# Gate and up as three float32r products with split weights and tokens, and the route's inverse roots as Newton rounds on VectorE

## The reference, cut to what matters

```python
def rmsnorm(x, w): return x * rsqrt(mean(x * x, -1, keepdims=True) + EPS) * w
h = rmsnorm(x, mlp_norm_w)
x = x + (silu(h @ Wgate) * (h @ Wup)) @ Wdown          # 128 -> 512 -> 128

# second mixture of experts, on x = layernorm of the sum so far
xn = (x - mu) * rsqrt(var + LN_EPS) * gamma + beta
probs = softmax(xn @ Wr + br); scores, idx = top_k(probs, 2)   # 8 experts
```

## Time and profile before

| what | us |
|---|---|
| runs: median (lowest to highest of 3) | 1336.76 (1336.28 to 1343.72) |
| the profiled execution's own time | 1339.15 |
| its span, first to last instruction | 1336.8 |
| PE busy in the span | 1201.7 |
| DVE busy in the span | 914.6 |
| ACT busy in the span | 829.8 |
| POOL busy in the span | 505.1 |
| mean granted TensorE clock | 0.958 |

### The profile page before, as it was taken

The page is one execution under the profiler, slowest core; times in us unless marked ns, Lnnn a source line. Parts: engine busy times, 40 slices in busy tenths (PEclk is TensorE's granted clock), DMA queues, the critical chain, the costliest instruction groups (busy, mean ns, idle before and its releaser), DMA issues. The chain is left out here.

```text
span 1336.8 us, 26862 instructions
## 1 busy us (share of the span) xinstructions
PE 1201.7 (90%) x7787; PEld 913.1 (68%) x7787; DVE 914.6 (68%) x3538; ACT 829.8 (62%) x2478; POOL 505.1 (38%) x619
## 2 busy tenths in 40 slices
PE   6999999999999998699975999999996989199990
PEld 4766676666667665499963777777774656199990
DVE  6788888888888775444436888888873666244445
ACT  5898888888989885244432565566554666044440
POOL 2111324142424232455542343433432376545550
PEclk9999999999999999799997999999997999599995
DMA  9100000000000000222221000000000011222226
GB/s 294 49 2 1 12 7 11 7 13 8 16 5 13 8 11 5 80 67 71 71 77 41 17 16 17 16 1 1 1 1 1 13 40 40 79 61 71 70 73 195
DMA packets 54443, 52.91 MB, mean 40 GB/s; under 512 B 7341, under 2 KB 43098, under 8 KB 54330
## 3 DMA queue, kind: packets, MB, share of 16 engines
q1 hardware_dynamic: 36320, 29.39, 7.7%
q0 software_dynamic: 8928, 17.84, 4.0%
q10 hardware_dynamic: 9082, 4.33, 1.1%
HBM read 29.48 MB, written 22.05 MB: 39 GB/s over the span
## 5 line engine op out<-in xcount | busy, mean ns | idle before, releaser
L1356 ACT ACTIVATE prob<-prob,negmax 128x256 f32<-128x256 f32 (+3 forms) x512 | 283.2, 556 | 37.5 <-DVE negmax L1450 37.5
L1450 DVE CUSTOM_DVE_ANT_0 prob<-bank,mask 128x256 f32<-128x256 f32 (+3 forms) x512 | 224.6, 480 | 36.8 <-PE bank L1166 34.4
L1529 POOL TENSOR_TENSOR Vs<-Vh_sb,rinv 128x512 f32<-128x512 f32 x64 | 66.7, 1042 | 355.9 <-DVE rinv L1428 355.9
L1052 POOL DMA_INDIRECT expert_out<-f_x_yb,f_x_to x142 | 136.8, 963 | 153.4 <-DVE f_x_yb L1040 131.0
L1178 PE MATMUL bank<-prob,Vs 128*64 128x512 f32 (+3 forms) x1024 | 153.6, 443 | 2.9 <-POOL Vs L1529 2.8
L680 POOL DMA_INDIRECT expert_in<-f_xn,f_slot x128 | 126.4, 987 | 46.2 <-issue 30.8
L984 PE MATMUL bank<-f_x_xbT,W_sb 128*128 128x256 f32 x568 | 138.6, 388 | 1.6 <-DVE f_x_xbT L1020 1.5
L1005 ACT ACTIVATE f_x_hid<-bank,cols 128x256 f32<-128x256 f32 x144 | 63.8, 475 | 91.4 <-PE bank L984 91.4
L984 PEld LDWEIGHTS bank<-f_x_xbT,W_sb 128*128 128x128 f32 x568 | 104.6, 194 | 14.8 <-DVE f_x_xbT L1020 2.6
L1178 PEld LDWEIGHTS bank<-prob,Vs 128*64 128x64 f32 x1024 | 64.2, 137 | 72.7 <-issue 62.9
L1005 ACT ACTIVATE prob<-bank,cols 128x256 f32<-128x256 f32 x140 | 62.1, 474 | 82.8 <-PE bank L984 82.8
(11 more groups left out here) (263 smaller groups left out, 3169.1 us busy)
## 6 DMA issues: line engine op xcount, KB each, us to landing
f_x_xb<-expert_in SPq DMA_DIRECT2D x73, 130.0 KB, 2.2
b_crows<-expert_out SPq DMA_DIRECT2D x16, 256.0 KB, 2.8
c_crows<-expert_out SPq DMA_DIRECT2D x16, 256.0 KB, 4.2
expert_out<-f_x_yb,f_x_to POOLq DMA_INDIRECT x142
expert_in<-fill ACTq DMA_DIRECT2D x16, 130.0 KB, 3.6
x_sb<-in_L_attn_a_x_dram SPq DMA_DIRECT2D x8, 256.0 KB, 6.4
W_sb<-in_L_ffn_W_dram SPq DMA_DIRECT2D x1, 2048.0 KB, 10.0
expert_in<-f_xn,f_slot POOLq DMA_INDIRECT x128, 2.4
```

The source lines that it names most:

```text
L1052: pool.indirect_dma_start(yg, bass.IndirectOffsetOnAxis(ap=self.to[:, t:t + 1], axis=0), self.yb[:, t, :], None).then_inc(self.stored[t], 16)
L1356: nc.scalar.activation(mine, mine, ACT.Exp, scale=-1.0, bias=negmax[:, g % 2, i, a:a + 1], accum_out=rowsum[:, g % 2, i, a:a + 1]).then_in ...
L1450: nc.vector.tensor_tensor_reduce(out=prob[:, g % 2, a, columns(i)], in0=score_bank(i, a), in1=mask[:, T - width[i]:], scale=-1.0, scalar=H ...
```

## The change

In the MLP stage:

- Gate and up become `matmul3` on float32r parts. The weights are split once, at the start of the stage, by four DVE instructions; ACT's `evacuate` writes the high part of the tokens, and DVE makes the low part in a new step `low_x(b)`, for row 0 before the loop and for row b + 1 between `gated(b,2)` and `gated(b,3)`. PE's `turn` and the start of a row wait for the low part instead of the high one.
- The two roots of a row leave POOL. DVE computes them in `dve_power`, directly behind `dve_base`: a start value from the bits of the base (a shift, then a multiply-add on integers), and three Newton rounds of three instructions each, on 128x8 elements, each instruction waiting for the one before. DVE's first `gated` of the next row stands behind them.

```diff
+            def dve_power(self, dve, b, u):
+                base = self.power[:, u, 2:4, :]
+                y = [self.root[:, k, :, :] for k in range(2)]
+                step = START + b * self.ROOT_STEPS
+                dve.wait_ge(self.base, START + 2 * b + 2)
+                nc.vector.tensor_scalar(self.root_bits[:, :, :], base.bitcast(i32), 1, None,
+                                        ALU.logical_shift_right).then_inc(self.rooted, 1)
+                dve.wait_ge(self.rooted, step + 1)
+                nc.vector.tensor_scalar(y[0].bitcast(i32), self.root_bits[:, :, :], -1.0, float(0x5F3759DF),
+                                        ALU.mult, ALU.add).then_inc(self.rooted, 1)
+                for r in range(self.ROUNDS):
+                    done = step + 2 + 3 * r
+                    out = self.power[:, u, 4:6, :] if r == self.ROUNDS - 1 else y[(r + 1) % 2]
+                    dve.wait_ge(self.rooted, done)
+                    nc.vector.tensor_tensor(self.root_square[:, :, :], y[r % 2], y[r % 2],
+                                            ALU.mult).then_inc(self.rooted, 1)
...
+                    ins.then_inc(self.rooted if r < self.ROUNDS - 1 else self.rstd, 1)
+                dve.sem_inc(self.rooted, 1)
...
-                            nc.tensor.matmul(bankG[c % 2][:, :], Wgate_sb[:, c * P:(c + 1) * P], xnT[:, b % 2, :],
-                                             start=True, stop=True).then_inc(gate_done, 1)
+                            f = slice(c * P, (c + 1) * P)
+                            matmul3(bankG[c % 2][:, :], Wgate_hi[:, f], Wgate_lo[:, f], xnT_hi[:, b % 2, :],
+                                    xnT_lo[:, b % 2, :]).then_inc(gate_done, 1)
...
                         turn(0)
+                        pe.wait_ge(gate_up_low, 2)
                         for b in range(B):
-                            pe.wait_ge(xnT_ready, START + b + 1)
+                            pe.wait_ge(xnT_lo_ready, START + b + 1)
...
+                        for high, full in ((Wgate_hi, Wgate_sb), (Wup_hi, Wup_sb)):
+                            nc.vector.tensor_copy(high[:, :], full[:, :]).then_inc(gate_up_high, 1)
...
+                            nc.vector.tensor_tensor(low[:, :], full[:, :], high[:, :],
+                                                    ALU.subtract).then_inc(gate_up_low, 1)
                         route.dve_begin(dve)
+                        def low_x(b):
+                            dve.wait_ge(xnT_ready, START + b + 1)
+                            nc.vector.scalar_tensor_tensor(
+                                out=xnT_lo[:, b % 2, :], in0=bankT[:, :], scalar=mlp_norm_col, in1=xnT_hi[:, b % 2, :],
+                                op0=ALU.mult, op1=ALU.subtract).then_inc(xnT_lo_ready, 1)
...
                             route.norm.dve_base(dve, b, slot_of(b))
+                            route.norm.dve_power(dve, b, slot_of(b))
...
                             gated(b, 2)
+                            if b < LAST:
+                                low_x(b + 1)
                             gated(b, 3)
...
-                            route.norm.pool_power(pool, b - 1, slot_of(b - 1))
...
-                        route.norm.pool_power(pool, LAST, slot_of(LAST))
```

More of the change, by code:

```diff
@@ L309, in __init__ @@
                     self.base, self.terms = sem(name + "_base_ready", at), sem(name + "_terms_ready", at)
-                    self.of_dve = (self.stats, self.moments, self.xn, self.base, self.terms)
-                self.of_pool = (self.pool_step, self.rstd, *[s for s in (self.sum, self.htok) if s is not None])
+                    self.rooted = sem(name + "_root_step", at)
+                    self.root = sb(name + "_root", [P, 2, 2, NT], at=at)
+                    self.root_square = sb(name + "_root_square", [P, 2, NT], at=at)
+                    self.root_error = sb(name + "_root_error", [P, 2, NT], at=at)
+                    self.root_bits = sb(name + "_root_bits", [P, 2, NT], i32, at=at)
+                    self.of_dve = (self.stats, self.moments, self.xn, self.base, self.terms, self.rstd, self.rooted)
+                self.of_pool = () if lean else (
+                    self.pool_step, self.rstd, *[s for s in (self.sum, self.htok) if s is not None])
             def tiles(self, b, where=None):
@@ L361, in dve_base @@
                                         ALU.add).then_inc(self.base, 1)
[L363 to L367, removed]
+            ROUNDS = 3
+            ROOT_STEPS = 2 + 3 * ROUNDS
@@ new lines, in dve_power @@
+            def dve_power(self, dve, b, u):
[14 more added lines that the diff above has]
+                                            ALU.mult).then_inc(self.rooted, 1)
+                    dve.wait_ge(self.rooted, done + 1)
+                    nc.vector.scalar_tensor_tensor(out=self.root_error[:, :, :], in0=self.root_square[:, :, :],
+                                                   scalar=-0.5, in1=base, op0=ALU.mult,
+                                                   op1=ALU.mult).then_inc(self.rooted, 1)
+                    dve.wait_ge(self.rooted, done + 2)
+                    ins = nc.vector.scalar_tensor_tensor(out=out, in0=self.root_error[:, :, :], scalar=1.5, in1=y[r % 2],
+                                                         op0=ALU.add, op1=ALU.mult)
+                    ins.then_inc(self.rooted if r < self.ROUNDS - 1 else self.rstd, 1)
+                dve.sem_inc(self.rooted, 1)
@@ L2011, in mlp_stage @@
                 xn = sb("m_xn", [P, 2, NT, D], at=st)
-                xnT = sb("m_xnT", [P, 2, T], at=st)
+                xnT_hi, xnT_lo = sb("m_xnT_hi", [P, 2, T], f32r, at=st), sb("m_xnT_lo", [P, 2, T], f32r, at=st)
+                Wgate_hi, Wgate_lo = sb("Wgate_hi", [P, INTER], f32r, at=st), sb("Wgate_lo", [P, INTER], f32r, at=st)
+                Wup_hi, Wup_lo = sb("Wup_hi", [P, INTER], f32r, at=st), sb("Wup_lo", [P, INTER], f32r, at=st)
+                gate_up_high, gate_up_low = sem("m_gate_up_high", st), sem("m_gate_up_low", st)
+                xnT_lo_ready = sem("m_xnT_lo_ready", st)
                 silu = sb("silu", [P, 2, T], at=st)
@@ L2046, in hidden @@
                             pe.wait_ge(silu_ready, START + n - 1)
-                            nc.tensor.matmul(bankG[c % 2][:, :], Wgate_sb[:, c * P:(c + 1) * P], xnT[:, b % 2, :],
-                                             start=True, stop=True).then_inc(gate_done, 1)
+                            f = slice(c * P, (c + 1) * P)
+                            matmul3(bankG[c % 2][:, :], Wgate_hi[:, f], Wgate_lo[:, f], xnT_hi[:, b % 2, :],
+                                    xnT_lo[:, b % 2, :]).then_inc(gate_done, 1)
                             pe.wait_ge(act_ready, START + n - 1)
-                            nc.tensor.matmul(bankU[c % 2][:, :], Wup_sb[:, c * P:(c + 1) * P], xnT[:, b % 2, :],
-                                             start=True, stop=True).then_inc(up_done, 1)
+                            matmul3(bankU[c % 2][:, :], Wup_hi[:, f], Wup_lo[:, f], xnT_hi[:, b % 2, :],
+                                    xnT_lo[:, b % 2, :]).then_inc(up_done, 1)
                         def down(b):
@@ L2101, in evacuate @@
                             act.wait_ge(turned, START + b + 1)
-                            nc.scalar.activation(xnT[:, b % 2, :], bankT[:, :], ACT.Copy,
+                            nc.scalar.activation(xnT_hi[:, b % 2, :], bankT[:, :], ACT.Copy,
                                                  scale=mlp_norm_col).then_inc(xnT_ready, 1)
@@ L2135, in _ @@
                     def _(dve):
-                        begin(dve, act_ready, x_done, *route.of_dve, *experts.of_dve)
-                        route.dve_begin(dve)
+                        begin(dve, act_ready, x_done, xnT_lo_ready, *route.of_dve, *experts.of_dve)
+                        for high, full in ((Wgate_hi, Wgate_sb), (Wup_hi, Wup_sb)):
+                            nc.vector.tensor_copy(high[:, :], full[:, :]).then_inc(gate_up_high, 1)
+                        for k, (low, full, high) in enumerate(((Wgate_lo, Wgate_sb, Wgate_hi),
+                                                               (Wup_lo, Wup_sb, Wup_hi))):
+                            dve.wait_ge(gate_up_high, k + 1)
+                            nc.vector.tensor_tensor(low[:, :], full[:, :], high[:, :],
+                                                    ALU.subtract).then_inc(gate_up_low, 1)
+                        route.dve_begin(dve)
+                        def low_x(b):
[3 more added lines that the diff above has]
+                                op0=ALU.mult, op1=ALU.subtract).then_inc(xnT_lo_ready, 1)
                         def x_add(b):
```

3 lines of the change are left out of this document (2 added, 1 removed).

## The result

The changed kernel takes 1364.14 us (median of four runs, 1361.17 to 1367.53), the kernel before on the same chip 1337.09: ratio 1.0188 with a 95% interval of [1.0161, 1.0215], slower. The forecast was 1352 with a range to 1360; the direction came out, and the time is 12 us above it, beyond the range.

A forecast was written before the change was run, and what follows sets the result against it. A chain through several engines, not PE, was taken to bound the MLP rows. 1339.15 + 11.3 (rows +11.4, start -0.5, tail +0.4) + 4.4 for the clock = 1354.9, on the median's base 1352; range 1341 to 1360.

The forecast's parts named there:

- The bound: MLP rows: a chain through several engines sets each row at 13.30 us; PE is merely nearly as long.
- Products: Gate and up on PE: a triple saves 0.17 us, one per row on the path; N to x_add becomes 8.63.
- N: Moment in each row when DVE comes to the normalising step: 4.50 us behind x_add before, 6.80 forecast.
- the rival with a triple no cheaper: Gate and up: a triple takes 1.29 us, N to x_add is 0.6 longer, total 1356; chance 0.05.
- Roots: DVE before gated(b,0): eleven dependent steps at 0.20 us, 2.20 in all; everything behind moves by 2.30.
- Low part of the tokens: DVE between gated(b,2) and gated(b,3): one instruction per row, 0.75 us, hidden while DVE waits for PE.
- Start: Weight split and row 0: PE's first product 1.2 us later, triples then save; net -0.5, between -1.5 and +2.5.
- Tail: Row 7's slots and scatters: +0.4 us, since DVE's root takes 2.4 from L360 to N instead of POOL's 2.0.
- Clock: PE's pauses in MLP rows: clock falls cost 1.1 us in four of seven intervals, +4.4, ends 0 and 13.
- clock falls in every row: MLP rows: the case of a clock fall in each row, left out of the range 1341 to 1360.

The follow-up runs named there:

- the products alone: Against the changed kernel, the roots go back to POOL and the float32r triples stay: 1335.78 us, ratio 0.9977.
- the filled pause: Against the changed kernel, ten unread float32r products in rows 1 to 7 between gate and up of chunk 2: 1351.53 us, ratio 1.0095.
- the roots alone: Against the kernel before, the Newton roots on DVE as in the change, gate and up left as float32 products: 1350.13 us, ratio 1.0091.
- the one with the sum later: Against the changed kernel, POOL's addition of z to x for the last row moved behind its next wait: 1362.16 us, ratio 1.0169.
- the exponential first and the pause filled: Against the products alone, ACT's exponential ahead of the update of x, and five unread products before the next row's transposes: 1338.0 us, ratio 0.9994.

## Why the prediction was wrong

The forecast before rounding was 1352.5, and 1364.1 came: 11.7 more. The profiled execution accounts for 6.3 of them. Against the working its seven intervals are 3.6 longer, the start 1.45 and the tail 0.2, behind the scatters 1.65 came, and the part outside the span is 0.6 shorter. The other 5.4 lie between that execution and the median: I carried over -2.39, but the profiled execution of the changed kernel was its fastest run, and the median lies 2.97 above it.

**The bound: right.** The rows are set by a chain through all engines and not by PE. The products alone took 6 us off PE's busy time in the seven intervals and nothing off their sum.

**Products: right.** N to x_add was put at 8.63. It is 8.59 and 8.66 in the two intervals of the changed kernel without a fall, and 8.60 to 8.84 in the whole rows of the filled one. In the rival with a triple no cheaper the 3.9 for row 0 does not follow from its rows: eight triples at 1.29 instead of 0.69 are 4.8, which makes that rival 1357.

**Roots: right.** The step was put at 0.20 and is 0.20; N was put at 6.80 behind x_add and is 6.82. The sum of the intervals without the clock was put at 108.3, +11.4; the pause filled gives 109.33, +12.4. The five whole rows there are 15.44 to 16.07 long, where I had put 15.43 for each. The Trainium skill ("VectorE: DVE Perf Modes", section "The DRAIN you can't avoid") finds, on eight copies, that a semaphore behind each costs nothing extra. That does not carry over to tiles this small: a step would then be its duration, 0.17 here, and it is 0.20, while the two independent bases L365 and L366 lie 0.08 apart (1107.54 and 1107.62).

**Low part of the tokens: right.** It takes 0.74, and N to x_add is as forecast with it, so it is hidden.

**Start: wrong by 1.45.** Forecast -0.5, measured +0.95, inside its ends of -1.5 and +2.5. I had left out that POOL's addition runs beside DVE's second subtraction, which costs 1.07 there (1.75 against 0.68). The Trainium skill has this in "SBUF — State Buffer", section "Who interferes with whom": a VectorE instruction with two inputs in SBUF and a GpSimd instruction that reads SBUF exclude each other, and the one that starts second waits for the whole of the other. The traces agree nearly: POOL began at 1024.54 and DVE, at 1024.63, was the one to wait, for 1.07 where the rule gives 1.21, up to POOL's end at 1025.84. With the addition moved away the 1.07 are gone. So PE's first product came 0.65 later than forecast (1.85 against 1.2). The other 0.8 is row 0 itself: from its first product to x_add it took 13.44 where it took 14.34, 0.9 less instead of 1.7. Why was not tried.

**Tail: nearly right.** +0.4 forecast, +0.6 measured; but behind the scatters 1.65 more was lost, for which there was no term (0.66 of it by the clock, 0.51 by a later landing).

**Clock: this is the step that failed.** The place, the cause and the price of a short fall were right: PE pauses in front of up of chunk 2, and a short fall costs 0.9 to 1.4 of a row (1.1 forecast). The size was not. "I take 1.1 in four of seven intervals: +4.4" became five intervals, one of them with a long fall that took 3.2: 7.0 in the profiled execution and 10.2 in another with the same rows. I had priced the transposes and one gate product at half clock, and had put logits and down, as the worst case, at 1.9 in all. When the clock stays down through up of chunk 3, logits and down as well, down alone takes 1.80 more (5.64 against 3.84). The ends I gave, 0 and 13, hold both sums. By the medians the filled pause gives back 12.6 us, 8.2 more than the 4.4 that I had put down, of the 11.7 by which the forecast was off; the profiles show 2.6 of these 8.2 in the rows. The range did not hold it: it left out "clock falls in every row", which is nearly what came. With the clock's own upper end the range would have reached 1361 (1339.15 + 11.3 + 13 - 2.39), and with the start's as well 1364. The Trainium skill ("TensorE: Matmul & The Clock Gate", section "A second HAM failure mode: psum-queue depth-cycling") says of another kernel that short pauses between groups of matmuls make the clock swing. The runs agree in kind, since filling the pause holds it at 1.00; the page gives no price for it on a chain.

The products helped the fall along, and I had put them down as pure gain. They end gate of chunk 2 sooner, so that PE waits 1.9 to 2.6 us instead of the 1.3 to 1.7 of the roots alone. The roots alone cost 12.2 us by their ratio, the products alone gain 3.1, and the two together cost 25. Whether the longer wait or the shorter products around it make the difference was not separated.

**What stays open.** Which row is hit was not settled, but the traces say more than I used. In the changed kernel and the one with the sum later, the same rows ran fourteen times. In the six where PE waited 2.51 to 2.63 us in front of up of chunk 2, the clock fell every time; in the eight where it waited 1.87 to 2.17, four times. And in the row behind each of the three at 0.73 the wait was 1.87: down ends late there. In the changed kernel the next row's first product then starts only 0.28 ahead of x_add (1139.20 and 1139.48), where it started 0.99 ahead one row before (1119.78 and 1120.77), and so PE reaches the wait later.

Of the 12.6 us between the medians of the changed kernel and of the filled pause, the profiles place 7.0 in the rows. The 3.7 us ahead of the first x_add lie in common code, and whether they belong to the change was not tried. Nor was it tried why the median of the changed kernel lies 3 us above its profiled execution. Its two longer runs (1366.51 and 1367.53) have a mean granted clock of 0.941 and 0.939, its two shorter ones (1361.17 and 1361.78) 0.945 and 0.944, so this may be the clock again; no trace of the longer ones shows where.

## What to carry to other kernels

Where the rows are a chain through several engines, a cheaper matmul buys nothing by itself, and every dependent small step put in front of work that others wait for costs its spacing, 0.20 us here, per row. Before moving such a chain, list how long PE will then wait: pauses of 1.9 to 2.6 us in the middle of dense products were followed by half clock in ten of the fourteen rows of two kernels here, those of 1.3 to 1.7 with the roots alone in none of seven, and the products behind the pauses are on the chain too. When gains vanish, look for the queue with the least slack in a row: here it was POOL's, with a wait for transfers in front of the next row's root; without that wait the seven intervals fell from 96.97 to 88.91 us.

## What the runs showed of the hardware that I had not expected

- Unread products made a kernel faster: 70 more of them in PE's pauses, and 12.6 us less by the medians, with a clock that stayed at 1.00 in the rows.
- A subtraction of two 128x512 tensors in DVE takes 0.68 to 0.69 alone and 1.75 beside an addition of two such tensors in POOL. Where POOL starts second, POOL is the slower one: 1.72 in the kernel with the exponential first and the pause filled, against 1.30 in the changed one.

```profile
1023.74 0.68 DVE L2188 TENSOR_TENSOR Wup_lo<-Wup_sb,Wup_hi 128x512 fp32r<-128x512 f32 x1
1023.83 1.72 POOL L1681 TENSOR_TENSOR x_sb<-x_sb,z_sb 128x512 f32<-128x512 f32 x1 [1.24 <-DMA spare<-z_sb]
```

- The first x_add stands between 1033.9 and 1041.3 us in the profiles of these kernels, mostly by differences in the earlier stages, whose code is the same. Clean rows of one program agree between profiles to some 0.1 us (the first interval is 14.55, 14.57 and 14.55 in three kernels with these rows), the sum over rows with falls only to 3 us (116.31 and 119.58), the total only to several.
